# Last stage of a five-part transformer kernel: scores in 64x32 tiles, values in 64x64 tiles, one sine operation, value transfers two at a time, new orders of the work

## The chip, the cores and the metric

The kernel runs on one core of a Trainium2 chip. The metric is the time of one execution on the device in microseconds. Three runs of the kernel before gave a median of 4817.93 us (4815.92 to 4821.29).

## The reference

The input `x` is 16 sequences of 256 tokens with 128 features, in f32. Four blocks follow each other, each `x + attention(norm(x)) + ffn(norm(x))`. The change touches the second half of the last one alone (stage `L3f`), which has six layers:

```python
def attn_layer(x, Wqkv, qs, ksc, Wo):          # 16 heads of 64, INNER = 1024
    q, k, v = split(x @ Wqkv)
    q = l2norm(q) * qs;  k = l2norm(k) * ksc
    q = q * cos * scale + rotate_half(q) * sin * scale
    k = k * cos / scale + rotate_half(k) * sin / scale
    # windows of 32 tokens; each looks at its own 32 keys and the 32 before them
    sim = einsum('bhwie,bhwje->bhwij', bq, bk2) * 8.0      # 32 x 64 per head and window
    attn = softmax(where(mask, -max, sim))
    out = einsum('bhwij,bhwje->bhwie', attn, bv2)
    return out @ Wo
for i in range(6):
    x = attn_layer(shift_tokens(x), ...) + x
    x = ffn_layer(shift_tokens(x), ...) + x     # layer norm, 128 -> 2 x 341, gelu gate, -> 128
```

## The kernel before

Stages `L0`, `L1`, `L2`, `L3a` and `L3f` run one after the other on the one core. In `L3f` a unit `u` is one sequence in one layer, 6 x 16 = 96 units. A unit has two tiles `t` of 128 tokens. All matmuls are in f32; the profile has two records of a weight load and two of a matmul for each of them, one for each pass.

Each engine has an order of its work written out by hand in `pe(i)`, `act(i)`, `dve(i)` and `pool(i)`, for two units at a time: `i` counts pairs, and one call of each function issues what belongs to units from `2i - 1` to `2i + 4`. The engines meet in semaphores alone (`wait_ge`, `then_inc`). So the work runs as a software pipeline whose period is one value of `i`. SyncE's queue (`sp(k)`) moves the values and loads weights.

What a unit does, with the functions that the change and the prediction name:

- TensorE `project` makes q, k and v in twelve pieces of 128 x 512 (`"q0a"` is q, tile 0, first half) into three PSUM banks in turn.
- ScalarE `squared`, VectorE `sums` and `bounded`, ScalarE `length` and VectorE `norm` make the l2 norm and write q and k to `raw`.
- GpSimd `sine`, `cosine` and `add` rotate them in place. `sine` multiplies the two halves of each head crosswise, in two operations of 512 elements; `cosine` and `add` are one operation of 1024 each.
- TensorE `turn_qk` transposes four 128 x 128 pieces, ScalarE `turned` copies them out: k to `kT`, q to `qz`. `qz` holds each pair of heads twice as wide as needed: one head's 64 rows have values in 32 columns, the other's in the next 32, and the rest is zero from the start (a memset). So one matmul of 128 rows and 64 columns of weights gives both heads of a pair for one window of 32 queries.
- TensorE `scores` makes eight pairs times four windows of these, on two column tiles of 64.
- VectorE `hidden` (mask), `top` (maximum), `below` (difference), ScalarE `exponent`, VectorE `total`, `share` and `scale` are the softmax, on 1024 elements a partition.
- TensorE `turn_p` transposes, ScalarE `spread` copies in four pieces to `pT`, again with zeros between the heads.
- SyncE moves the values from `v2` to `vw` by windows, 16 transfers a unit (`sp`); TensorE `values` multiplies them with `pT`, 32 matmuls a tile, each with 128 rows, 64 columns of weights and 64 moving columns.
- ScalarE `output`, TensorE `project_out`, VectorE `residual`, then the feed-forward part: `centre`, `variance`, `centred`, `root`, `normal`, `affine`, `ffn_gate`, `gelu`, `ffn_up`, `gated`, `ffn_out`, `ffn_done`.

Two functions of stage L1 serve as comparison further on. Its `values` (lines 896 and 899) puts out to four column tiles of 32 in turn, its `scores` (line 857) takes from four row tiles of 32 in turn:

```python
for i in range(RG):   # RG = 4, rows(i) is the i-th group of 32 partitions
    p.matmul(PS[rows(i), 4, t * P:(t + 1) * P], vz[:, b, t, i, u * RW:(u + 1) * RW], sT[:, i, ...], ...)
    mm = p.matmul(PS[:, i, ...], km[rows(i), b, u, ...], qT[rows(i), b, ...], start=True, stop=True)
```

## Time and profile before

| | |
|---|---|
| median of three runs | 4817.93 us (4815.92 to 4821.29) |
| span of the profiled execution, first to last instruction | 4799.2 us |
| TensorE busy, of the span | 4554.0 us (95%) |
| VectorE | 3761.7 us (78%) |
| GpSimd | 3692.6 us (77%) |
| ScalarE | 3501.1 us (73%) |

The profile is of one execution. Its own time outside the span is not recorded; the median of the runs lies 18.7 us above the span. PE is TensorE's matmuls, PEld its weight loads, DVE is VectorE, ACT ScalarE, POOL GpSimd, SP SyncE. Each matmul's duration contains the way through the array, so a duration is longer than the time from one matmul to the next. The chain of waits is the chain of work that ended last, followed back from the end. `qz` stands as L3f_qz, and so on; PSUM is `ps`.

### The profile page before, as it was taken

What the parts mean: (1) busy time and instruction counts of PE and PEld (TensorE: products, weight loads), DVE (VectorE), ACT (ScalarE), POOL (GpSimd) and SP (SyncE); (2) the same over time, 40 slices, a digit from 0 to 9 for tenths busy, and PEclk for the clock granted to TensorE, in tenths of its full rate; (3) what the DMA queues carried; (4) which work ended last, traced back from release to release, by engine and by line L of the source; (5) the groups of instructions that cost most, each with busy time, mean ns of one, the idle gap of its engine ahead of it and who ended that gap; (6) DMA issues with size and microseconds to landing.
All of it is one profiled execution on the core that took longest, in us unless ns stands there. A gap on an engine that the chain in (4) does not pass through costs nothing.

```text
span 4799.2 us, 114895 instructions
## 1 busy us (share of the span) xinstructions
PE 4554.0 (95%) x44512; PEld 3128.6 (65%) x44512; DVE 3761.7 (78%) x5226; ACT 3501.1 (73%) x6738; POOL 3692.6 (77%) x2336
## 2 busy tenths in 40 slices
PE   7998999987887799999999999999999999999997
PEld 5666768874443466666666666666666666666665
DVE  6776556658999688888888888888888888888885
ACT  3454756557775688888888888888888888888885
POOL 2222334438998999999999999999999999999993
PEclk9898999998999999999999999999999999999998
DMA  2000000004332222232222322232322322322222
GB/s 79 1 2 1 2 1 1 1 1 168 150 142 106 55 63 63 56 85 70 54 67 65 75 68 55 68 75 61 68 64 67 76 53 66 80 64 63 62 56 52
DMA packets 164292, 289.06 MB, mean 60 GB/s; under 512 B 44063, under 2 KB 61351, under 8 KB 159655
## 3 DMA queue, kind: packets, MB, share of 16 engines
q1 hardware_dynamic: 162310, 281.46, 22.3%
q8 instruction: 357, 5.85, 0.5%
q14 instruction: 185, 1.51, 0.1%
q10 hardware_dynamic: 1440, 0.24, 0.0%
HBM read 90.22 MB, written 2.62 MB: 19 GB/s over the span
## 4 chain that ended last, share of the span: by engine, by line
PE 59%; ACT 3%; issue 2%; DVE 1%; POOL 1%; ACTq 0%; DVEq 0%; POOLq 0%
PE ps L2559 18%; PE ps L2614 8%; PE ps L2588 8%; PE ps L2572 7%; PE ps L2627 7%; PE ps L2601 3%; PE ps L2669 3%; PE ps L2660 3%; PE ps L2653 3%; ACT L3f_pT L2820 2%; PE ps L2634 1%; PE ps L2640 1%; ACT L3f_kT L2803 1%; POOL L3f_t L3155 0%; POOL L3f_raw L3172 0%
## 5 line engine op out<-in xcount | busy, mean ns | idle before, releaser
L3155 POOL TENSOR_TENSOR L3f_t<-L3f_raw,L3f_rot 128x512 f32<-128x512 f32 x768 | 1007.7, 1334 | 268.3 <-DVE L3f_raw L2971 268.3
L2559 PE MATMUL ps<-L3f_wqkv,all_z 128*128 128x512 f32 x2304 | 1133.7, 601 | 12.8 <-DVE L3f_raw L2971 11.7
L3172 POOL TENSOR_TENSOR L3f_raw<-L3f_raw,L3f_t 128x1024 f32<-128x1024 f32 x384 | 961.4, 2504 | 3.8
L3164 POOL TENSOR_TENSOR L3f_raw<-L3f_raw,L3f_rot 128x1024 f32<-128x1024 f32 x384 | 953.8, 2484 | 3.8
L2971 DVE TENSOR_TENSOR L3f_raw<-ps,L3f_ri 128x512 f32<-128x512 f32 x768 | 495.6, 682 | 231.9 <-ACT L3f_ri L2778 230.2
L2954 DVE TENSOR_REDUCE L3f_ss<-L3f_sqr 128x8 f32<-128x512 f32 x768 | 507.8, 681 | 163.2 <-ACT L3f_sqr L2768 160.8
L2572 PEld LDWEIGHTS ps<-all_ident,L3f_raw 128*128 128x128 f32 x3072 | 358.7, 141 | 320.7 <-issue 282.8
L2559 PEld LDWEIGHTS ps<-L3f_wqkv,all_z 128*128 128x128 f32 x2304 | 385.2, 191 | 221.0 <-issue 151.5
L2572 PE MATMUL ps<-all_ident,L3f_raw 128*128 128x128 f32 x3072 | 472.3, 276 | 49.1 <-ACT L3f_kT L2803 27.1
L2820 ACT ACTIVATE L3f_pT<-ps 64x512 f32<-64x512 f32 x768 | 453.2, 590 | 83.9 <-PE ps L2601 75.9
L2768 ACT ACTIVATE L3f_sqr<-ps 128x512 f32<-128x512 f32 x768 | 449.9, 599 | 76.5 <-PE ps L2559 71.7
L2799 ACT ACTIVATE L3f_qz<-ps 64x512 f32<-64x512 f32 x768 | 451.5, 588 | 59.7 <-PE ps L2572 55.2
L2614 PEld LDWEIGHTS ps<-L3f_pT,L3f_vw 128*64 128x64 f32 x12288 | 377.4, 139 | 95.4 <-issue 50.9
L2614 PE MATMUL ps<-L3f_pT,L3f_vw 128*64 128x64 f32 x12288 | 404.0, 225 | 7.5 <-ACT L3f_pT L2820 7.5
L2588 PEld LDWEIGHTS ps<-L3f_kT,L3f_qz 128*64 128x64 f32 x12288 | 375.2, 138 | 52.5 <-issue 52.5
L2588 PE MATMUL ps<-L3f_kT,L3f_qz 128*64 128x64 f32 x12288 | 399.1, 223 | 0.0
L2803 ACT ACTIVATE L3f_kT<-ps 128x512 f32<-128x512 f32 x384 | 231.9, 604 | 164.7 <-PE ps L2572 163.5
L2627 PE MATMUL ps<-L3f_oT,L3f_wo 128*128 128x256 f32 x1536 | 349.3, 381 | 2.6 <-ACT L3f_oT L2830 2.6
L2627 PEld LDWEIGHTS ps<-L3f_oT,L3f_wo 128*128 128x128 f32 x1536 | 292.9, 191 | 84.5 <-issue 46.2
L3014 DVE TENSOR_TENSOR L3f_sm<-L3f_sm,L3f_sl 128x1024 f32<-128x1024 f32 x192 | 339.3, 1767 | 0.0
L2281 POOL TENSOR_TENSOR L3a_db_x<-L3a_dx,L3a_Bs 128x1024 f32<-128x1024 f32 x128 | 299.4, 2358 | 1.3 <-DMA L3a_Bs<-L3a_rows 1.1
L1916 PE MATMUL ps<-L3a_hc,all_ident 128*128 128x512 f32 x512 | 248.7, 633 | 39.0 <-DVE L3a_hc L2189 22.5
(333 smaller groups left out, 8702.0 us busy)
## 6 DMA issues: line engine op xcount, KB each, us to landing
L3f_vw<-L3f_v SPq DMA_DIRECT2D x1344, 128.0 KB, 2.4
L3a_Bs<-L3a_rows SPq DMA_DIRECT2D x16, 2048.0 KB, 7.1
L3a_Cs<-L3a_rows SPq DMA_DIRECT2D x16, 2048.0 KB, 11.6
L3f_vw<-L3f_v SPq DMA_DIRECT2D x192, 64.0 KB, 2.1
L3f_wqkv<-in_L_ffn_Wqkv SPq DMA_DIRECT2D x24, 256.0 KB, 2.9
L3f_wqkv<-in_L_ffn_Wqkv SPq DMA_DIRECT2D x6, 512.0 KB, 3.6
L3f_wo<-in_L_ffn_Wo SPq DMA_DIRECT2D x48, 64.0 KB, 2.3
out<-all_x SPq DMA_DIRECT2D x8, 256.0 KB, 3.6
```

Source lines behind the costliest of these rows:

```text
L2559: p.matmul(PS[:, j % 3, :], Z[:, u % NSEQ, t * P:t * P + P], w, start=True, stop=True).then_inc(proj.sem)
L2572: mm = p.transpose(PS[:, 3, c * P:c * P + P], raw[:, t, (4 * g + c) * P:(4 * g + c + 1) * P], ident[:, :])
L2588: mm = p.matmul(PS[r, 6 + w // 2, a * KEYS:(a + 1) * KEYS], qz[:, t, a, w, :, :].rearrange("p h q -> p (h q)"), kT[:, a, t * P + w * WIN:t ...
L2614: mm = p.matmul(PS[r * HD:(r + 1) * HD, 4 + c // 2, (c % 2) * 256 + w * HD:(c % 2) * 256 + (w + 1) * HD], vw[:, u % 2, t * NW + w, a * HD: ...
L2627: mm = p.matmul(PS[:, 4, 0:SEQ], wo[:, c, h, :], oT[:, :, c, :, h, :], start=(c + h == 0), stop=(c + h == PAIRS // 2))
L2799: op = a.activation(qz[r, t, 4 * g:4 * g + 4, :, half, :], src[r, :, :].rearrange("p c (w q) -> p c w q", q=WIN), ACT.Copy)
L2820: op = a.activation(pT[half * HD:(half + 1) * HD, t, r:2 * PAIRS:2, :, half, :], PS[r * HD:(r + 1) * HD, 4:6, :].rearrange("p b (n w h q) ...
L2954: v.tensor_reduce(ss[:, 0, i * UH:(i + 1) * UH], heads(sqr[:, i % 2, :]), AX.X, ALU.add).then_inc(ss_in.sem)
L2971: v.tensor_tensor(heads(raw[:, t, g * UNIT:(g + 1) * UNIT]), heads(PS[:, RING.index(x) % 3, :]), ri[:, i * UH:(i + 1) * UH].unsqueeze(2).b ...
L3155: op = g.tensor_tensor(t[:, :, to], r[:, :, fr], w[:, 1, to].unsqueeze(1).broadcast_to((P, H, WIN)), ALU.mult)
L3164: g.tensor_tensor(r, r, w[:, 0, :].unsqueeze(1).broadcast_to((P, H, HD)), ALU.mult).then_inc(cosined.sem)
L3172: g.tensor_tensor(r, r, t, ALU.add).then_inc(rotated.sem)
```

## The change

- `qz` becomes `qT` without zeros: `turned` copies q in one operation. `scores` makes, for each pair, window and head, one matmul with 64 rows, 32 columns of weights and 64 moving columns: 64 a tile instead of 32. Window `w` puts out to column group `w`, head `h` takes row group `h` and writes to bank `6 + h`. The mask is laid out accordingly, and `below` writes `sm` in the order pair, head.
- `pT` has no zeros either: `spread` is one copy of 1024 elements. `values` makes, for each head, window and half, one matmul with 64 rows, 64 columns of weights and 32 moving columns: 64 a tile instead of 32, on two row and two column groups. `oT` and `project_out` follow its layout.
- The memsets of `qz` and `pT` go.
- `sine` is one operation of 1024 elements that reads the two halves of a head in reversed order.
- SyncE waits before each value transfer from the third on until the transfer two before it has landed, with two semaphores in turn.
- The orders of all four engines are written anew from the same functions, and `i` runs from -4 to N / 2 + 2 instead of -2 to N / 2.

```diff
-        qz = self.sb("qz", [P, TILES, PAIRS, NW, 2, WIN])
+        qT = self.sb("qT", [P, TILES, PAIRS, P])
-        pT = self.sb("pT", [P, TILES, 2 * PAIRS, 2, 2, WIN])
-        oT = self.sb("oT", [P, TILES, PAIRS // 2, NW, 2, WIN])
+        pT = self.sb("pT", [P, TILES, PAIRS, P])
+        oT = self.sb("oT", [P, TILES, 2, PAIRS // 2, P])
...
+                pieces = [(part, shift, half, w) for part, shift in ((WIN, 0), (0, 1)) for half in range(2) for w in range(NW)]
+                for n, (part, shift, half, w) in enumerate(pieces):
+                    landed = v_put[k % 2][n % 2]
+                    if n >= 2:
+                        s.wait_ge(*landed.at(k // 2, 16 * (n // 2) - 1))
...
                 for a in range(PAIRS):
                     for w in range(NW):
-                        r = slice(w % 2 * HD, w % 2 * HD + HD)
-                        mm = p.matmul(PS[r, 6 + w // 2, a * KEYS:(a + 1) * KEYS], qz[:, t, a, w, :, :].rearrange("p h q -> p (h q)"),
-                                      kT[:, a, t * P + w * WIN:t * P + w * WIN + KEYS], start=True, stop=True)
+                        for h, (r, _) in enumerate(halves):
+                            mm = p.matmul(PS[w * WIN:(w + 1) * WIN, 6 + h, a * KEYS:(a + 1) * KEYS], qT[r, t, a, w * WIN:(w + 1) * WIN],
+                                          kT[r, a, t * P + w * WIN:t * P + w * WIN + KEYS], start=True, stop=True)
...
                 for c in range(PAIRS // 2):
                     for w in range(NW):
-                        for r in range(2):
-                            a = 2 * c + r
-                            mm = p.matmul(PS[r * HD:(r + 1) * HD, 4 + c // 2, (c % 2) * 256 + w * HD:(c % 2) * 256 + (w + 1) * HD],
-                                          vw[:, u % 2, t * NW + w, a * HD:(a + 1) * HD],
-                                          pT[:, t, w // 2 * PAIRS + a, w % 2, :, :].rearrange("p h q -> p (h q)"), start=True, stop=True)
+                        for to, n in halves:
+                            a = 2 * c + n
+                            for h, (r, _) in enumerate(halves):
+                                mm = p.matmul(PS[to, 4 + h, c * P + w * WIN:c * P + (w + 1) * WIN], vw[r, u % 2, t * NW + w, a * HD:(a + 1) * HD],
+                                              pT[r, t, a, w * WIN:(w + 1) * WIN], start=True, stop=True)
...
-                    for half in range(2):
-                        r = slice(half * HD, half * HD + HD)
-                        op = a.activation(qz[r, t, 4 * g:4 * g + 4, :, half, :], src[r, :, :].rearrange("p c (w q) -> p c w q", q=WIN), ACT.Copy)
+                    op = a.activation(qT[:, t, 4 * g:4 * g + 4, :], src, ACT.Copy)
...
-                for r in range(2):
-                    for half in range(2):
-                        op = a.activation(pT[half * HD:(half + 1) * HD, t, r:2 * PAIRS:2, :, half, :],
-                                          PS[r * HD:(r + 1) * HD, 4:6, :].rearrange("p b (n w h q) -> p (b n) w h q", w=2, h=2, q=WIN)[:, :, :, half, :], ACT.Copy)
-                op.then_inc(pT_in.sem)
+                a.activation(pT[:, t, :, :].rearrange("p a q -> p (a q)"), PS[:, 4:6, :].rearrange("p b n -> p (b n)"), ACT.Copy).then_inc(pT_in.sem)
...
-                for half in range(2):
-                    to, fr = slice(half * WIN, (half + 1) * WIN), slice((1 - half) * WIN, (2 - half) * WIN)
-                    op = g.tensor_tensor(t[:, :, to], r[:, :, fr], w[:, 1, to].unsqueeze(1).broadcast_to((P, H, WIN)), ALU.mult)
-                op.then_inc(sined.sem)
+                g.tensor_tensor(t.rearrange("p h (b e) -> p h b e", b=2), r.rearrange("p h (b e) -> p h b e", b=2)[:, :, ::-1, :],
+                                w[:, 1, :].rearrange("p (b e) -> p b e", b=2).unsqueeze(1).broadcast_to((P, H, 2, HD // 2)), ALU.mult).then_inc(sined.sem)
...
-        for i in range(-2, N // 2 + 1):
+        for i in range(-4, N // 2 + 3):
```

## Rows read from the trace of the kernel before

**Rows 1.** The page: busy time of each engine.
```profile
PE 4554.0 (95%) x44512; PEld 3128.6 (65%) x44512; DVE 3761.7 (78%) x5226; ACT 3501.1 (73%) x6738; POOL 3692.6 (77%) x2336
```
**Rows 2.** Chain of waits, L3f: start us, us, what; period marks and bursts.
```profile
1677.77 3.45 PE ps L2627 x16
...
3064.14 3.45 PE ps L2627 x16
3067.59 0.44 PE ps L2572 x4
...
3071.49 2.02 PE ps L2588 x64
...
3079.15 2.02 PE ps L2614 x64
3081.16 1.87 PE ps L2588 x64
...
3130.08 3.45 PE ps L2627 x16
...
4712.15 3.73 PE ps L2627 x16
```
**Rows 3.** Busy time by stretch, one period: length, PE, PEld, DVE, ACT, POOL, clock, DMA.
```profile
3064.14:3130.08 65.94, 65.28 (x715) 44.84 (x715) 54.30 (x78) 53.85 (x102) 60.00 (x33) 1.00 0.34 85
```
**Rows 4.** Waits of POOL from 1700 to 4600 us: us in total, times, longest.
```profile
POOL L3f_t L3155 <- DVE L3f_raw L2971: 251.9, 171, 2.9
```
**Rows 5.** Timeline of TensorE's matmuls in stage L1: start us, us.
```profile
541.67 0.40 PE L899 MATMUL ps<-L_sT,L_onz 128*32 128x128 f32 x8
541.89 0.40 PE L896 MATMUL ps<-L_sT,L_vz 128*32 128x128 f32 x8
...
545.04 1.17 PE L857 MATMUL ps<-L_qT,L_km 32*128 32x128 f32 x32
```
**Rows 6.** Line 896 in 30 ns: records under way, PE (x), PEld (x).
```profile
541.42:541.46 0.03, 0.02 (x4) 0.03 (x4) 1.00 0.00 0
```
**Rows 7.** Weight loads by line, ns min/median/max: 32, 64 and 128 columns.
```profile
L896 PEld LDWEIGHTS ps<-L_sT,L_vz x512: 106/110/110, 480.3 to 634.4; 128*32 128x32 f32 x171
L2614 PEld LDWEIGHTS ps<-L3f_pT,L3f_vw x12288: 132/138/227, 1627.7 to 4766.1; 128*64 128x64 f32 x199
L857 PEld LDWEIGHTS ps<-L_qT,L_km x512: 181/187/333, 472.9 to 627.5; 32*128 32x128 f32 x171
```
**Rows 8.** Groups by line, ACT, the period of rows 3: busy us, mean ns.
```profile
L2820 ACT ACTIVATE L3f_pT<-ps 64x512 f32<-64x512 f32 x16 | 9.4, 590 | 1.7 <-PE ps L2601 1.5
L2799 ACT ACTIVATE L3f_qz<-ps 64x512 f32<-64x512 f32 x16 | 9.4, 588 | 1.2 <-PE ps L2572 1.1
...
L2830 ACT ACTIVATE L3f_oT<-ps 128x1024 f32<-128x1024 f32 x4 | 4.1, 1026 | 0.8 <-PE ps L2614 0.7
```
**Rows 9.** Timeline of POOL, the period before: start us, us; undisturbed operations.
```profile
3019.55 2.51 POOL L3155 TENSOR_TENSOR L3f_t<-L3f_raw,L3f_rot 128x512 f32<-128x512 f32 x2
...
3024.34 2.36 POOL L3164 TENSOR_TENSOR L3f_raw<-L3f_raw,L3f_rot 128x1024 f32<-128x1024 f32 x1
```
**Rows 10.** Groups by line, VectorE, the period of rows 3.
```profile
L3014 DVE TENSOR_TENSOR L3f_sm<-L3f_sm,L3f_sl 128x1024 f32<-128x1024 f32 x4 | 7.1, 1782 | 0.0
```
**Rows 11.** SP: one unit's issues, landing time, and its queue's waits.
```profile
3033.73 10.24 SPq L2510 DMA_DIRECT2D L3f_vw<-L3f_v  x16
...
L3f_vw<-L3f_v SPq DMA_DIRECT2D x1344, 128.0 KB, 2.4
...
SPq L2504 <- PE ps L2614: 1317.8, 88, 18.0
SPq L2510 <- ACT L3f_v L2787: 484.4, 44, 11.5
```
**Rows 12.** Chain of waits at the stage's start, and ACT in the last 99 us.
```profile
1556.91 3.47 DVE L3f_pT L3203
...
L2820 ACT ACTIVATE L3f_pT<-ps 64x512 f32<-64x512 f32 x20 | 11.8, 591 | 5.4 <-PE ps L2601 5.2
```

More of the change, by code:

```diff
@@ L2785, in value @@
                 if u >= 2:
-                    a.wait_ge(*v_put[u % 2].all(u // 2 - 1))
+                    for e in range(2):
+                        a.wait_ge(*v_put[u % 2][e].all(u // 2 - 1))
                 a.activation(v2[:, u % 2, int(x[1]), "ab".index(x[2]), :], PS[:, j % 3, :], ACT.Copy).then_inc(v_out.sem)
@@ L2872, in gelu @@
                     a.preload_act_table_set(EXP_LN)
+            value(2 * i + 1, "v0b")
+            squared(2 * i + 1, "q1a")
+            turned(2 * i, 1, 2)
+            squared(2 * i + 1, "q1b")
+            squared(2 * i + 1, "k1a")
+            length(2 * i + 1, "q1")
+            output(2 * i - 1, 0)
+            turned(2 * i, 1, 3)
+            squared(2 * i + 1, "k1b")
+            spread(2 * i - 1, 1)
+            length(2 * i + 1, "k1")
+            turned(2 * i + 1, 0, 0)
+            value(2 * i + 1, "v1a")
@@ new lines, in act @@
+            exponent(2 * i, 0)
+            turned(2 * i + 1, 0, 1)
+            affine(2 * i - 2)
+            value(2 * i + 1, "v1b")
+            squared(2 * i + 2, "q0a")
+            squared(2 * i + 2, "q0b")
+            output(2 * i - 1, 1)
+            squared(2 * i + 2, "k0a")
+            exponent(2 * i, 1)
+            length(2 * i + 2, "q0")
+            turned(2 * i + 1, 0, 2)
+            squared(2 * i + 2, "k0b")
+            turned(2 * i + 1, 0, 3)
+            centred(2 * i - 1)
@@ new lines, in act @@
+            length(2 * i + 2, "k0")
+            turned(2 * i + 1, 1, 0)
+            root(2 * i - 1)
+            value(2 * i + 2, "v0a")
+            turned(2 * i + 1, 1, 1)
+            squared(2 * i + 2, "q1a")
+            spread(2 * i, 0)
+            squared(2 * i + 2, "q1b")
+            value(2 * i + 2, "v0b")
+            turned(2 * i + 1, 1, 2)
+            output(2 * i, 0)
+            turned(2 * i + 1, 1, 3)
+            length(2 * i + 2, "q1")
+            exponent(2 * i + 1, 0)
+            spread(2 * i, 1)
@@ L3071, in dve @@
             bounded(2 * i + 3, "q0")
-            scale(2 * i + 1, 1)
+            sums(2 * i + 3, "k0a")
+            normal(2 * i)
             norm(2 * i + 3, "q0a")
+            share(2 * i + 1, 1)
             norm(2 * i + 3, "q0b")
-            normal(2 * i)
             land(2 * i - 1, range(FINAL - 1))
```

319 lines of the change are left out of this document (136 added, 183 removed).

## The prediction

> **What bounds the kernel now.** I read the page first: its busy shares [rows 1] show a kernel in which TensorE is busy 95% of the span and three other engines over 70%, so no share alone names the bound. The changed stage L3f runs from about 1.56 ms to the end, and there the chain of waits repeats itself: the same 16-record piece of `project_out` stands at 3064.14 and 3130.08 us [rows 2], so one pass of the written-out orders (two sequences, a "period" below) takes 65.94 us. From 1677.77 to 4712.15 us that is 3034.38 / 65.94 = 46.0 periods. The busy time by stretch [rows 3] says what fills one: TensorE 65.28 us at a granted clock of 1.00, GpSimd 60.0, VectorE 54.3, ScalarE 53.85. TensorE idles 0.66 us; GpSimd idles 5.9, and the waits [rows 4] show it waiting for VectorE's `norm` and for nothing else. So TensorE's work sets the period, and GpSimd stands 9% behind it.
>
> **Scores.** A record is one of the two passes that an f32 matmul takes. Now `scores` makes 32 matmuls, 64 records, with 64 weight columns and 64 moving columns, on two column tiles in turn. Four such bursts stand in a period: three of 2.02 us and one of 1.87 [rows 2], 7.93 us in all. The short one follows `values`, which has the same tile shape, so entering a shape costs 0.15 us, and in the steady burst a record takes 1.87 / 64 = 29.2 ns; the two tiles together take 58.4 ns for a round of two. After the change there are 64 matmuls, 128 records, of 32 weight and 64 moving columns, and eight tiles (two row groups, four column groups) come in turn. Do eight work at once? The L1 stage is the nearest row [rows 5]. `L896` and `L899` use four column tiles with 128 moving columns: 8 records from 541.67 to 541.89 us, 27 ns a record, 110 ns a round of four. A pass of 128 columns by itself takes the same 110 ns (`L2572`, four in 0.44 us [rows 2]): four column tiles cost no more than one. `L857` uses four row tiles: 32 records of 128 columns in 1.17 us, 37 ns each with entry and exit instead of 110, so row tiles overlap as well. And tiles can start close together: four matmul records and four weight loads begin inside one stretch of 30 ns [rows 6], about 7 ns from tile to tile, which puts eight of them into some 56 to 60 ns. A round of eight should then take what a round of two takes now, 58.4 ns. 128 / 8 = 16 rounds make 0.93 us, with the entry 1.09. Four bursts: 7.93 to 4.36, **-3.6 us a period**. Bounds: the best is this very value, since a tile's own 64 columns can't go faster; the worst is that no average below the 27.3 ns of [rows 5] can be had, 128 x 27.3 = 3.5 us a burst.
>
> **Values.** The same doubling: 64 records become 128, the moving side shrinks from 64 to 32 columns, but each load still brings 64 weight columns, now to four tiles. What a load costs is in the durations [rows 7]: 110 ns for 32 columns, 138 for 64, 187 for 128, so 0.8 ns a column on top of a fixed part, and 64 columns are some 52 ns. A tile that needs new weights for each record thus can't have a record more often than every 52 ns, whatever its moving side is. I take the round at today's 58.4 ns: 128 / 4 = 32 rounds make 1.87 us, with the entry 2.02. Four bursts: 8.08 to 8.08, **0**. Bounds: 32 rounds at half, 29 ns, are 0.93 + 0.15 = 1.09 us (-3.7 a period), if the load hides; 3.5 us a burst (+5.9 a period) if 27.3 ns is the least.
>
> The skill has a rule that promises more here than the rows do: the Trainium skill, "TensorEngine Tiling (Array Packing)", section "Theoretical Speedup", gives up to twofold for each dimension of 64 or less, by which `values`, going from column tiles to row and column tiles with the same total work, would halve. By it the sum below would be about 4.53 ms, by the load durations it is 4.65 ms. Its warning beside this, not to take a tiling factor from a dimension that is small already (section "Instruction Overhead"), is on the side of the durations.
>
> **ScalarE.** In a period sixteen half-height copies of `qz` (9.4 us) become eight of full height, at today's 0.59 4.7 us, and sixteen of `pT` (9.4 us) become four of 1024 elements at 1.03, 4.1 us [rows 8]: 53.85 to 44 us, -9.9. ScalarE isn't the bound, so I count nothing, but latencies on TensorE's side shrink: `spread` from 2.4 us to 1.03. At most TensorE's 0.66 us of idle time can be won by it.
>
> **VectorE.** `hidden`, `below`, `total`, `scale` keep their 1024 elements; `below` now writes in another order, which no row prices. It costs from 0 to, if it took the price of the dearest of them twice (`L3014`, 1.78 [rows 10]), some +1.8 x 4 = 7 us: 54.3 would be 61.5, still behind TensorE's 61.7. I take 0, since its element count stays.
>
> **GpSimd.** The two 512-element products of `sine` take 2.51 us together when undisturbed, a 1024-element one 2.36 [rows 9]. One operation saves 0.15, eight times a period: -1.2, GpSimd 60.0 to 58.8. The reversed order of halves is in no row; at worst it gives that back, for more than 2.51 nothing in the rows speaks. It is hidden now, and it matters as the next bound.
>
> **Value transfers.** Sixteen transfers are issued in 10.24 us, one each 0.64, and one takes 2.4 us to land [rows 11]. With two in flight a pair costs 2.4 to 2.5: 8 x 2.45 = 19.6 us a sequence, +9.4. Behind the waiting SP instruction stand the next sequence's transfers and the layer's weight loads. SP waits 1318 + 484 = 1802 us in 88 sequences now, 20.5 each, so it has room for 9.4. The burst issued at 3033.73 serves `values` at 3079.15, 45 us later [rows 2, 11]; 19.6 is in time. It would decide only from 31 us a sequence, 3.9 us a pair. The weights of the next layer, issued behind them, could come up to 4 us later, five times in all: I take 0, at most 20 us in the whole run.
>
> **Orders.** The new orders hold the same operations. TensorE at 65.28 - 3.57 = 61.7 us needs GpSimd to be busy 58.8 of 62.4, and VectorE to feed it: GpSimd's idle share shrinks from 5.9 to 3.6 us a period. The price of an order is in no row of before. It lies between -0.66 us (no idle time left) and +3.6 us (the whole gain given back); I keep today's 0.66 us idle, the nearest row.
>
> **Head and tail.** The `pT` memset of 3.47 us is on the chain at 1556.91 [rows 12] and goes: -3.5. In the last 99 us the twenty `pT` copies take 11.8 us and there is little else to cover them; five full ones take 5.2. I take some 60% of them for being on the chain, -4, and three score bursts -3. Together -10.
>
> **Sum.** Period 61.7 + 0.66 = 62.4, 3.54 less; x 46.0 = -163; head and tail -10: -173. The profiled execution has a span of 4799.2; the median of the runs is 4817.93, so 18.7 us lie around the span. 4799.2 - 173 + 18.7 = **4645 us**.
>
> **Rivals.**
> - *A: as summed*, 4645, own range 4600 (0.5 us less idle and a cheaper entry) to 4700 (1.2 us a period more waiting). Chance 0.56.
> - *B: `values` gains too.* The load hides behind the other tiles' work. Then TensorE needs 61.7 - 3.7 = 58.0, GpSimd's 58.8 takes over as bound, and with 1.2 us of its waiting left the period is 60.0: 5.9 x 46 + 10 = 283 less, 4534. For it: a round of four column tiles already covers four loads. Against: the durations of [rows 7]. 0.12.
> - *C: a least time for each record; slower.* Twice as many records of half the work cost twice as much if TensorE can't average below some 27 ns. Place: both bursts. 3.5 + 3.5 us instead of 2.02 + 2.02, less the 0.15 of the short one: (28.0 - 16.0) = +12 a period, x 46 = +550, so 5360 us with the 10 of head and tail. It decides from a mean of 16.0 / 1024 = 15.6 ns a record (the sum above has 12.44 / 1024 = 12.1). For it: no stretch of the trace is denser than 27.3 ns. Against: that stretch is explained by its 128 columns over four tiles, and starts 7 ns apart show [rows 6]. 0.15. The Trainium skill, "TensorE: Matmul & The Clock Gate", section "Wait — 56ns, not 53.3ns?", speaks for this rival: matmuls never start less than about 25 ns apart, however small; by its figure the sum would be some 5.25 ms. Its own section "The mechanism" has tiles start about 4 ns apart, and the 30 ns stretch of this trace agrees with that one.
> - *D: no more than four tiles at once*, the most that a row shows. Scores then take 32 rounds, 1.87 + 0.15, and TensorE's work stays: the change does nothing to the bound; head and tail remain, 4810. 0.09.
> - *E: the new orders bring waits* between VectorE, GpSimd and TensorE that take back 2.5 to 4.5 us a period: 4760 to 4850. For it: GpSimd at 94% of the period instead of 91%. 0.08.
>
> **Numbers.** The likeliest gives 4645. From 4530 (B) to 4815 (D, half of E) lie 0.56 + 0.12 + 0.09 + 0.04 = 0.81; C is left out above. A difference of 0.2%, 10 us, is about what this measurement can tell. Faster: A, B, a third of D and E, 0.74. Same: 0.07. Slower: C and the rest, 0.19.
>
> **What would show it.** The period between two 16-record `project_out` pieces: 62.4. `scores` in the chain: 128 records in about 1.1 us (3.5 under C, 2.0 under D). `values`: 2.0 (1.1 under B). ScalarE 44 us a period, GpSimd 58.8. TensorE's waits still small; under B and E, waits for GpSimd's or VectorE's tiles at `L2572` and `L2559`. No wait for `v_put`. I am wrong above all if eight small tiles don't overlap, since nothing in this trace has run eight.

## The result and the profile after

The change made the kernel slower: 5036.25 us (median of 4, 5035.66 to 5068.0) against 4816.93, ratio 1.0481, 95% interval 1.0453 to 1.0508. The forecast was 4645, in a range of 4530 to 4815: the time went the other way, to a place outside that range. One run of e11 below (5209 us) and one of e13 (8369 us) took far longer than the rest at a lower granted clock; the ratios leave them out, and the medians hardly move by them. The profiled execution has a span of 5034.3 us; at the same marks as in [rows 2] its period is (4955.75 - 1670.23) / 46 = 71.4 us, 5.5 more than before and 9.0 more than forecast.

The page of the changed kernel, busy time of each engine and the queue that brings instructions (packets, MB, share of 16 engines' span); it answers to [rows 1]:

```profile
PE 4554.6 (90%) x69088; PEld 3037.0 (60%) x69088; DVE 3839.6 (76%) x5225; ACT 3259.4 (65%) x5964; POOL 3674.7 (73%) x1951
...
q8 instruction: 549, 8.99, 0.7%
```

TensorE executes half as many records again and is idle 10% of the span, 5% before. Before, the same queue moved 357 packets and 5.85 MB. A packet is 8.99 MB / 549 = 16 KB. TensorE's compiled program has 8995584 bytes, 549.05 times 16 KB, in instructions of 64 bytes each: the queue brings TensorE's instructions, 256 in a packet. A packet's time is 0.7% x 5034.3 x 16 / 549 = 1.0 us.

Busy time by stretch of the changed kernel, one of the better periods (columns as in [rows 3]):

```profile
3027.79:3097.19 69.40, 63.71 (x1228) 42.46 (x1227) 56.74 (x78) 48.98 (x86) 60.57 (x26) 1.00 0.26 59
```

Even here TensorE idles 5.7 us, for 0.66 before, at a granted clock of 1.00. The chain of waits of the changed kernel shows two places. First the bursts of small tiles (start us, us, what):

```profile
3083.46 2.00 PE ps L2619 x128
...
3089.07 1.41 PE ps L2591 x91
...
3114.51 1.39 PE ps L2591 x84
3115.89 1.23 issue
3117.12 0.34 PE ps L2591 x12
3117.46 1.91 PE ps L2562 x4
3119.38 2.00 PE ps L2619 x128
```

`values` (L2619) takes 2.00 us for 128 records, as forecast for it (2.02). `scores` (L2591) takes 1.41 where nothing is wrong, and at 3115.89 it has a hole of 1.23 us *inside one burst*, released by nothing that the profile shows. The chain lists only some of a burst's records (the trace has all 128), so a burst is to be read by its times here, not its counts. A "hole" is a step of over 0.6 us from the start of one record of a burst to the start of the next. Measured in the trace from a burst's first record to the next operation, over the 192 bursts, in us:

```
          scores: shortest   mean   holes over 0.6 us   values: median   mean   holes
before               1.97    2.01                   0             2.02   2.03       0
after                1.40    1.89                  47             2.00   2.09       3
```

Second, right behind it, the gelu and its table loads. The chain of waits of the changed kernel, and ScalarE's timeline over the same time:

```profile
3121.44 1.11 PE ps L2657 x2
...
3123.16 1.01 ACT L3f_oT L2830
...
3124.20 1.28 ACT L2814
3125.49 1.06 ACT L3f_sm L2814
3126.55 0.48 ACT L3f_v L2792
...
3127.05 1.28 ACT L2780
...
3131.40 0.70 ACT L3f_gg L2870
...
3132.14 1.57 PE ps L2664 x2
```

```profile
3119.17 1.28 ACT L2866 ACT_TABLE_LOAD   x1
3122.58 0.69 ACT L2870 ACTIVATE L3f_gg<-ps,L3f_b 128x512 f32<-128x512 f32 x1 [2.12 <-PE ps L2657]
...
3124.20 1.28 ACT L2814 ACT_TABLE_LOAD   x1
...
3127.05 1.28 ACT L2780 ACT_TABLE_LOAD   x1
...
3128.58 1.28 ACT L2782 ACT_TABLE_LOAD   x1
...
3130.11 1.28 ACT L2870 ACT_TABLE_LOAD   x1
3131.40 1.26 ACT L2870 ACTIVATE L3f_gg<-ps,L3f_b 128x512 f32<-128x512 f32 x2
3132.68 1.28 ACT L2872 ACT_TABLE_LOAD   x1
```

The new ScalarE order puts `exponent` and `length` between the first gelu and the other two. These functions live in different activation tables, so ScalarE loads six tables a period in place of two; two of the six stand inside `length`, whose two functions (L2780, L2782) now get a load each. TensorE fills the time behind the first gelu with `project_out` and then stands still at `ffn_up`'s second part (L2664) until the second gelu comes. Its timeline, with the idle time before the operation in brackets:

```profile
3124.95 3.62 PE L2631 MATMUL ps<-L3f_oT,L3f_wo 128*128 128x256 f32 x16
3132.14 1.57 PE L2664 MATMUL ps<-L3f_fn,L3f_w 128*128 128x512 f32 x2 [3.57 <-ACT L3f_gg L2870]
```

The waits of the changed kernel from 1700 to 4850 us (total, times, longest) show it in sum, 3.5 us in each of 44 periods; before TensorE never waited for a gelu:

```profile
PEld ps L2664 <- ACT L3f_gg L2870: 171.3, 44, 4.0
PE ps L2664 <- ACT L3f_gg L2870: 153.7, 44, 3.6
```

A third loss stands in no chain: what such a wait leaves behind. The trace has two levels of TensorE's granted clock, 1.2 and 2.4 GHz (0.50 and 1.00). The busy time by stretch, of the kernel before and of the changed one:

```profile
1700.00:4700.00 3000.00, 2968.86 (x32403) 2036.23 (x32404) 2480.44 (x3512) 2447.92 (x4590) 2731.29 (x1455) 1.00 0.28 66
```

```profile
1700.00:4850.00 3150.00, 2884.12 (x53945) 1894.15 (x53944) 2481.57 (x3400) 2158.57 (x3744) 2631.75 (x1056) 0.97 0.27 62
```

From 1600 us on, the clock rows of the trace have 209 us at the lower level in the changed kernel and 33 in the one before. 36 of the 45 stretches behind 1700 us begin within 2 us of the end of a wait for the second gelu. At half the clock up to half of the time is lost, so this part can be worth up to (209 - 33) / 2 = 88 us of the 219 that the change cost (an estimate: it takes TensorE to be busy all the while). The experiment e3 below shows it most clearly.

### The profile page after: what moved, and what is told of

Read it like the earlier page. It is cut to its first block, busy times and chain, and to the rows that moved or that the text cites. A ratio compares the mean times of both kernels' runs of the same rounds, so it can differ in the third digit from the quotient of the medians.

```text
span 5034.3 us, 162887 instructions
## 1 busy us (share of the span) xinstructions
PE 4554.6 (90%) x69088; PEld 3037.0 (60%) x69088; DVE 3839.6 (76%) x5225; ACT 3259.4 (65%) x5964; POOL 3674.7 (73%) x1951
## 3 DMA queue, kind: packets, MB, share of 16 engines
q8 instruction: 549, 8.99, 0.7%
## 4 chain that ended last, share of the span: by engine, by line
PE 50%; ACT 8%; issue 6%; DVE 4%; POOL 1%; ACTq 0%; DVEq 0%; POOLq 0%
PE ps L2562 19%; PE ps L2619 7%; PE ps L2575 6%; PE ps L2591 5%; PE ps L2631 3%; PE ps L2664 3%; PE ps L2604 3%; PE ps L2673 2%; DVE L3f_sm L3015 1%; PE ps L2657 1%; ACT L2870 1%; ACT L2780 1%; ACT L2814 1%; ACT L3f_oT L2830 1%; ACT L3f_sm L2814 1%
## 5 line engine op out<-in xcount | busy, mean ns | idle before, releaser
L3154 POOL TENSOR_TENSOR L3f_t<-L3f_raw,L3f_rot 128x1024 f32<-128x1024 f32 x384 | 941.2, 2451 | 510.7 <-DVE L3f_raw L2971 510.7
L2619 PEld LDWEIGHTS ps<-L3f_pT,L3f_vw 64*64 64x64 f32 x24576 | 380.5, 135 | 126.2 <-issue 114.5
L3015 DVE TENSOR_TENSOR L3f_sm<-L3f_sm,L3f_sl 128x1024 f32<-128x1024 f32 x192 | 451.0, 2349 | 0.1
L2619 PE MATMUL ps<-L3f_pT,L3f_vw 64*64 64x32 f32 x24576 | 404.2, 220 | 7.8 <-issue 4.9
L2591 PE MATMUL ps<-L3f_kT,L3f_qT 64*32 64x64 f32 x24576 | 302.0, 225 | 71.2 <-issue 69.5
L2591 PEld LDWEIGHTS ps<-L3f_kT,L3f_qT 64*32 64x32 f32 x24576 | 262.6, 105 | 148.6 <-issue 147.8
L2664 PE MATMUL ps<-L3f_fn,L3f_w 128*128 128x512 f32 (+1 forms) x288 | 196.0, 771 | 160.8 <-ACT L3f_gg L2870 160.8
L2802 ACT ACTIVATE L3f_qT<-ps 128x512 f32<-128x512 f32 x384 | 227.9, 593 | 166.9 <-PE ps L2575 161.2
L2981 DVE TENSOR_TENSOR ps<-ps,L3f_lmaskb 128x1024 f32<-128x1024 f32 x192 | 235.8, 1228 | 85.5 <-PE ps L2591 85.1
L3037 DVE SCALAR_TENSOR_TENSOR L3f_gg<-ps,L3f_b,L3f_gg 128x512 f32<-128x512 f32 x144 | 107.8, 749 | 248.7 <-PE ps L2664 248.4
```

The costliest lines, as they stand in the source:

```text
L2591: mm = p.matmul(PS[w * WIN:(w + 1) * WIN, 6 + h, a * KEYS:(a + 1) * KEYS], qT[r, t, a, w * WIN:(w + 1) * WIN], kT[r, a, t * P + w * WIN:t ...
L2619: mm = p.matmul(PS[to, 4 + h, c * P + w * WIN:c * P + (w + 1) * WIN], vw[r, u % 2, t * NW + w, a * HD:(a + 1) * HD], pT[r, t, a, w * WIN:( ...
L3015: v.tensor_tensor(x, x, sl[:, t, :].unsqueeze(2).broadcast_to((P, H, KEYS)), ALU.mult).then_inc(s_mul.sem)
L3154: g.tensor_tensor(t.rearrange("p h (b e) -> p h b e", b=2), r.rearrange("p h (b e) -> p h b e", b=2)[:, :, ::-1, :], w[:, 1, :].rearrange( ...
```

## The experiments

All times are medians; the kernel before, run beside them, had 4805 to 4817 us. The column "L3f" has the time from the first record of `project` in the changed stage to the end, in the one profiled execution of each kernel; before has 3243. It is a check on small differences: the stages ahead are the same in all kernels, yet the first `project` of L3f stands anywhere from 1547 to 1588 us.

| kernel | us | ratio to before (95%) | L3f | mean scores burst, holes |
|---|---|---|---|---|
| after | 5036 | 1.048 (1.045 to 1.051) | 3479 | 1.89, 47 |
| e1 after, gelus together | 4937 | 1.026 (1.022 to 1.030) | 3363 | 1.88, 42 |
| e2 after, orders of before | 4911 | 1.022 (1.019 to 1.026) | 3338 | 2.32, 86 |
| e3 before, orders of after | 5224 | 1.087 (1.084 to 1.090) | 3663 | |
| e15 e3, gelus together | 5065 | 1.054 (1.051 to 1.057) | 3509 | |
| e4 e2, transfers of before | 4886 | 1.017 (1.014 to 1.020) | 3326 | 2.32, 83 |
| e12 before, transfers of after | 4817 | 1.000 (0.998 to 1.002) | 3250 | |
| e11 before, one sine operation | 4808 | 0.998 (0.996 to 1.000) | 3240 | 2.00, 0 |
| e5 small scores alone | 4768 | 0.990 (0.987 to 0.993) | 3207 | 1.93, 52 |
| e6 small values alone | 4858 | 1.009 (1.006 to 1.012) | 3291 | 2.12, 12 |
| e7 e4, scores in late quarters | 5346 | 1.110 (1.106 to 1.113) | 3779 | 16 |
| e8 e5, scores in late quarters | 5306 | 1.101 (1.097 to 1.105) | 3756 | 0 |
| e9 e5, scores in early halves | 4850 | 1.008 (1.005 to 1.010) | 3294 | 38 |
| e10 e5, scores in early quarters | 5051 | 1.050 (1.046 to 1.053) | 3486 | 5 |
| e13 e5, bursts at good places | 4763 | 0.991 (0.988 to 0.993) | 3200 | 1.57, 7 |
| e14 e5, bursts at bad places | 4901 | 1.019 (1.017 to 1.022) | 3341 | 2.03, 58 |
| e16 e13, cheaper padding | 4733 | 0.984 (0.982 to 0.986) | 3173 | 1.63, 12 |

**The orders: e1, e2, e3, e15.** e1 changes two lines of ScalarE's order:

```diff
             gelu(2 * i - 1, 0)
+            gelu(2 * i - 1, 1)
+            gelu(2 * i - 1, 2)
             output(2 * i, 1)
             exponent(2 * i + 1, 1)
             value(2 * i + 2, "v1a")
             length(2 * i + 2, "k1")
-            gelu(2 * i - 1, 1)
-            gelu(2 * i - 1, 2)
```

> The changed kernel with the three gelu calls of a period next to each other again on ScalarE (the changed order has an exponent, a value copy and a length between the first and the second). Theory O (the new ScalarE order is the main loss): six table loads a period become two, 5.1 us of ScalarE, and TensorE's wait of some 9 us at ffn_up falls to under 4; the period of 71.5 us falls to 65 to 67, the time to 4770 to 4860 us. Theory T (the small tiles are the main loss, through more instructions): the wait moves but the time stays over 4980 us.

e2 has the functions of after and the four orders of before, e3 the reverse; both take the loop's range along. e15 is e3 with the edit of e1.

> The changed kernel (small tiles, one sine operation, transfers two at a time) with all four orders of before. Theory O: the loss is in the orders, so this lands at 4780 to 4830 us, near before, since the score bursts of the changed kernel take 1.89 us on average and so win next to nothing over the 2.01 of before. Theory T: over 4980 us. My prediction's mechanism, had the orders been harmless, would give 4645.

> The kernel before with the four new orders alone (large tiles, two sine operations, free transfers). Theory O: 4990 to 5080 us, as slow as the changed kernel or slower, with six table loads a period. Theory T: 4800 to 4850 us.

> The functions of before with the four new orders, but the three gelu operations side by side (as in the run of that name): the new orders on the large tiles without the added table loads. They cost 100 us in the changed kernel (5036 to 4937) and the rest of the new orders nothing there (4937 against 4911 with the old ones). Theory: most of the 409 us that the new orders cost on the large tiles is the table loads and what waits behind them: 4830 to 4950. Rival O (the new orders fit only the shorter ScalarE operations of the new tiles, since ScalarE has 54 us of work in 66 here): above 5000 even without the table loads.

Splitting the gelus costs 99 us in the changed kernel (5036 to 4937) and 159 on the large tiles (5224 to 5065). Not all of this is waiting. TensorE's timeline of e3, the same line ahead of the wait and behind it:

```profile
1781.04 1.02 PE L2660 MATMUL ps<-L3f_fn,L3f_w 128*128 128x512 f32 x2
...
1789.09 2.08 PE L2660 MATMUL ps<-L3f_fn,L3f_w 128*128 128x512 f32 x2 [3.57 <-ACT L3f_gg L2870]
```

The same two records take twice as long: from 1788.00 to 1794.80 us the granted clock is 0.50, and such a stretch stands in every period. From 1600 us on e3 has 346 us at the lower level and e15 104, the changed kernel 209 and e1 128. By the estimate used above the clock is up to 121 of the 159 us and up to 40 of the 99.

The rest of the new orders costs 26 us in the changed kernel (4937 against 4911) and 254 on the large tiles (5065 against 4811): rival O of the last text holds there. TensorE's waits from 1700 to 4600 us, first in e15, then in e1:

```profile
PE ps L2627 <- ACT L3f_oT L2830: 92.3, 41, 2.3
PE ps L2614 <- ACT L3f_pT L2820: 49.0, 41, 1.2
PE ps L2572 <- ACT L3f_qz L2799: 37.3, 40, 1.2
```

```profile
PE ps L2631 <- ACT L3f_oT L2830: 94.5, 42, 2.3
```

The waits for the copies of p and q are there with the large tiles alone, whose copies take longer. e1's wait for `output` costs less than it says, for e1 has 42 holes where e2, without that wait, has 86: while TensorE waits for an engine, its next instructions can arrive. All four times missed what was set: e1 came 77 us above its range, e3 144 above, e15 above theory's 4950 and in its rival's place, and e2 81 above. In e2 a hole can now be in `values` too (20 of 192, 3 in the changed kernel). The chain of waits of e2:

```profile
2030.08 1.99 PE ps L2619 x126
2032.07 0.46 issue
2032.53 0.24 PE ps L2619 x2
...
2051.03 0.67 PE ps L2591 x46
2051.70 1.99 issue
2053.69 1.38 PE ps L2591 x74
```

**Transfers and sine: e4, e12, e11.** e4 takes the wait for the transfer before last out of e2; e12 and e11 put the new transfers, and the new sine, into the kernel before and nothing else.

```diff
-                    if n >= 2:
-                        s.wait_ge(*landed.at(k // 2, 16 * (n // 2) - 1))
```

> As e2_old_orders, but the value transfers are issued without waiting for each other. If bursts of transfers hold up the fetch of TensorE's instructions, the gaps inside the score bursts grow and the time is 10 to 50 us above e2_old_orders. If waiting two by two has no effect on the rest, the two agree within 5 us.

> The kernel before with the one edit of the value transfers (two at a time on two semaphores each, in place of sixteen issued at once). By the difference of the two versions with old orders (4911 with the wait, 4886 without) it costs 0 to 30 us here; a rival in which fewer transfers at once leave the instruction packets more room gives 10 to 20 us less than before, but before has no idle stretch at such packets to win back.

> The kernel before with the one edit of the sine (one GpSimd operation for two halves). GpSimd is busy 60 of 66 us a period and behind TensorE. Theory: within 0.3% of before, 4795 to 4820; a rival in which GpSimd's rotation decides when the turns of q and k start gives 4750 to 4790, about 1 us a period.

e4 is 26 us faster than e2, and neither of the two outcomes that I had set (10 to 50 us slower, or within 5) came. In the kernel before the paced transfers cost 1 us. But of the 27 us between the two profiled executions of e2 and e4 15 lie ahead of L3f; inside the stage the transfers cost 12 us there (3338 against 3326) and 7 in the kernel before (3250 against 3243). So a small cost is likely, and that it arises with small tiles alone isn't shown. The sine is worth 7 us at most, 3 inside the stage, at the edge of what the measurement can tell.

**Which tile: e5, e6.** Both stand on e4. e5 puts the large value tiles back, with the small tiles' `scores`:

```diff
-                        for to, n in halves:
-                            a = 2 * c + n
-                            for h, (r, _) in enumerate(halves):
-                                mm = p.matmul(PS[to, 4 + h, c * P + w * WIN:c * P + (w + 1) * WIN], vw[r, u % 2, t * NW + w, a * HD:(a + 1) * HD],
-                                              pT[r, t, a, w * WIN:(w + 1) * WIN], start=True, stop=True)
+                        for r in range(2):
+                            a = 2 * c + r
+                            mm = p.matmul(PS[r * HD:(r + 1) * HD, 4 + c // 2, (c % 2) * 256 + w * HD:(c % 2) * 256 + (w + 1) * HD],
+                                          vw[:, u % 2, t * NW + w, a * HD:(a + 1) * HD],
+                                          pT[:, t, w // 2 * PAIRS + a, w % 2, :, :].rearrange("p h q -> p (h q)"), start=True, stop=True)
...
+                for r, half in halves:
+                    for b in range(2):
+                        op = a.activation(pT[r, t, b * PAIRS:(b + 1) * PAIRS, :, half, :],
+                                          PS[r, 4:6, :].rearrange("p c (n b w q) -> p (c n) b w q", b=2, w=2, q=WIN)[:, :, b, :, :], ACT.Copy)
```

e6 puts the large score tiles, `qz` and the old mask back and keeps the small values, with eight copies of a quarter each for the turned p.

> The orders and transfers of before, the one sine operation, scores in 64x32 tiles, but values again in 128x64 tiles with zero halves (64 large ones a burst, four copies out of the PSUM for the turned p). Theory F (TensorE runs dry of instructions: a scores burst is 128 weight loads and 128 matmuls, run off in a little over 1 us, and the next 16 KB of instructions land later than that): the scores burst keeps gaps of 1 to 2.5 us in a third or more of the bursts, and the time is that of the version with both kinds of small tiles and the old orders (4886) within 30 us: 4850 to 4915. Rival V (it is the small value tiles that lose the time, their doubled records make the instructions scarce for what follows): the gaps in scores all but vanish, the mean burst is near 1.4 us, and with 4 x 0.5 us a period won the time is 4690 to 4760.

> The orders and transfers of before, the one sine operation, values in 64x64 tiles without zero halves, but scores again in 128x64 tiles (64 a burst). Theory F: a values burst is now 256 instructions in 2.0 us, a little faster than the instructions come, so some bursts get a gap of up to 1 us but far fewer than the scores had; TensorE's work is that of before: 4815 to 4870. Rival V: the loss of the small tiles sits here, 4870 to 4920. A third view, that less ScalarE work alone helps, would give 4780 to 4810.

For e5 rival V is nearly right in the time, 4768 for its 4690 to 4760 and 118 us less than e4, and wrong in what the bursts do: it has them at 1.4 us, and 52 holes stay, more than a quarter of the bursts, as under F. The small value tiles bring nothing by themselves (2.00 us for 2.02) and double their share of the instructions. From e4 to e5 the scores bursts in sum fall from 444.6 to 370.4 us and the values bursts from 420.6 to 396.3, 98 of the 118. e6 is slower than before and inside F's range; 12 of its bursts of large scores have a hole, which none has in the kernel before, and 7 of its `values`; its eight small ScalarE copies are part of that, so its 49 us aren't the price of the tiles alone. e5 beats the kernel before by 1.0%.

**Are the holes a lack of instructions? e7 to e10.** The burst is issued in parts; only the placing differs. Late: the first part where the burst was, the others each behind a later operation. Early: the last part where the burst was.

```diff
-            scores(2 * i + 2, 0)
+            scores(2 * i + 2, 0, 0)
             project(2 * i + 3, "v0b")
+            scores(2 * i + 2, 0, 1)
             project(2 * i + 3, "q1a")
+            scores(2 * i + 2, 0, 2)
             project(2 * i + 3, "q1b")
+            scores(2 * i + 2, 0, 3)
```

> The version with the old orders and free transfers (4886), where each burst of 128 small scores is issued in four parts of 32 with another operation of TensorE between each two. The same instructions, only spread over more time. Theory F: no stretch of 256 instructions is run off in much under 2.5 us any more, so idle stretches of over 0.6 us inside scores fall from some 80 to under 20 and their total from some 170 us to under 60; what the later last part costs in waits for the masks is smaller: 4760 to 4840. Rival D (the records themselves are slow, by bank or by tile conflicts, wherever they stand): the parts add up to as much as the whole burst did, and the later scores come on top: 4886 to 4960.

> Small scores in four parts as in the run before it, and large values with zero halves as in the first of these runs: the lowest number of TensorE instructions with small scores. Theory F: as few gaps as with quarters and both small tiles or fewer, since values issue half as many instructions: 4720 to 4810, the fastest of these four. Rival D: 4880 to 4960.

> The version with small scores alone (4768), with each burst in two halves of 64. The second half stays where the burst was; the first (pairs 0 to 3, which need one copy fewer of the turned q and k) stands one or two operations of TensorE earlier, before a turn, a projection or the values. So the last score is no later than before, and a stretch of 256 instructions takes some 1.6 us in place of 1.1. Theory F: idle stretches of over 0.6 us inside scores fall from 52 to 15 to 35, and nothing else is late: 4700 to 4760. Rival L (what the run in late quarters lost was the price of any split, not of the later last part): above 4790.

> Small scores alone, in four parts of 32, the last of them where the burst was and the first three one operation each earlier (before the values of the other tile two and two). Theory F: under 15 idle stretches of over 0.6 us are left inside scores; the parts start up to 1.5 us earlier and may wait for the bank that the masks and maxima of the tile before still hold, up to 0.5 us a burst: 4680 to 4760. Rival L: above 4790, as in the late quarters (5306).

In the scores the holes went down, 83 to 16 in e7 and from 52 to 0, 38 and 5 in e8, e9 and e10, as F says but for e9, which it had at 15 to 35. Some only moved: `values` has 31 in e7 for 18 in e4, and 14 in e9 for none in e5, so e9 has 52 in all, as many as e5. The times went the other way. It isn't rival D: a part of 32 records takes 0.39 us in the median of e7, the four 1.56. Two more ends of the scores show. What the scores of e7 waited for and who waited for them (us, times):

```profile
  ACT L3f_qT L2814: 36.4, 48
who waited for it (us, times):
  DVE ps L2993: 729.5, 192
```

VectorE's mask waits 3.8 us for each late burst (729.5 / 192; in e4 it is 55.8 / 192 = 0.3). And what the scores of e10 waited for, besides issue:

```profile
  DVE L3f_sm L3013: 143.3, 47
  ACT L3f_kT L2820: 55.5, 41
  DVE all_z L3064: 47.8, 46
```

An early part waits for the bank that `below` of the tile before still reads (L3013), for the other one that the FFN's residual still reads (L3064), and for k. I had priced this at 0.5 us a burst at most; it is (143.3 + 55.5 + 47.8) / 192 = 1.3. My forecast for all four was wrong by 90 us and more. Rival L's number was met too. Its price of any split wasn't told apart from these waits; what the rows show is that a burst has a window, between the bank's release before it and the mask behind it, and that the spread parts reach beyond it on either side.

**The same instructions at other places: e13, e14.** A sharper test had to leave the order alone. In e5's compiled program I counted at which place each burst starts, in blocks of 256 TensorE instructions from the program's start:

```
start within the block     bursts   holes   mean burst, us
0 to 63                        49       8     1.76
64 to 127                      43       5     1.68
128 to 191                     49       3     1.56
192 to 255                     51      36     2.66
```

The same count gives the place at which each hole ends, and that is sharper still: all 52 holes of e5 end at place 195 or 196, and so do all 47 of the changed kernel, the 7 of e13, the 58 of e14 and the 12 of e16, wherever their bursts start. There TensorE goes over from one packet's instructions to the next's.

e13 pads a period with some 20 tiny matmuls to a multiple of 256 instructions, so that each burst keeps its place, and e14 is e13 but for one number, 47 where e13 has 30.

```diff
+                first = 30 if (u, x) == (0, "q0a") else 0
+                for n in range(first + (u >= 2) * {"q1b": (1 - u % 2) * 7, "k1b": (1 - u % 2) * (13 - u // 2 % 2)}.get(x, 0)):
+                    p.matmul(PS[0:WIN, j % 3, 0:2], ident[0:HD, 0:WIN], ident[0:HD, 0:2], start=True, stop=True)
                 p.matmul(PS[:, j % 3, :], Z[:, u % NSEQ, t * P:t * P + P], w, start=True, stop=True).then_inc(proj.sem)
```

> Small scores alone (4768) with some 20 tiny matmuls of 2 columns more a period (78 instructions), put ahead of projections whose bank they write first. They make a period of TensorE's program 8 times 256 instructions long, so that each of the four scores bursts of a period always starts at the same place within a 16 KB block of 256 instructions; 30 more of them at the very start choose the places: about 183, 134, 108 and 66. In the kernel without them 36 of the 52 bursts with an idle stretch over 0.6 us were among the 50 that start at 192 to 255, and few among those at 64 to 191. Theory F (a block that is asked for when the block before it is entered comes in 2 to 3 us after, and what is ahead runs out before only if the burst starts just behind that point): fewer than 15 such stretches in 192 bursts, the mean burst falls from 1.93 to 1.5 to 1.65 us, the tiny matmuls cost 10 to 25 us, the time is 4705 to 4760. Rival R (the stretches come from something else that only happens in bursts, such as the clock or tile changes): as many as before, 4775 to 4800.

> The same kernel as the run before it but for one number: 47 in place of 30 tiny matmuls at the very start, so that the bursts start at about 251, 202, 176 and 134 within a block. Theory F: the first two bursts of nearly every period have an idle stretch over 0.6 us, 65 to 95 in 192, the mean burst is 2.1 to 2.5 us and the time is 60 to 130 us above that of the run before. Rival R: the same time as the run before within 0.3%.

What the scores waited for, first in e13, then in e14:

```profile
  ACT L3f_qT L2803: 36.4, 48
  issue: 34.1, 134
```

```profile
  issue: 206.9, 227
  ACT L3f_qT L2803: 36.4, 48
```

17 tiny matmuls at the start of a stage, some 1 us of work, make 138 us of difference at the end, 140 inside L3f. 88 of them are the longer scores bursts (389.7 us in sum for 301.6); another 28 are 36 idle stretches in `turn_p`, of which e13 has none. In e14, 46 of the 49 bursts that start at 192 to 223 have a hole, and none of the 95 that start at 64 to 191. The order and the work are the same, so rival R is out: it had the two within 0.3%.

The packets say how a hole comes about. In e14, 371 of the stage's 374 packets start only after TensorE has gone over place 195 into the block ahead of theirs, 1.2 us after that in the median. Where a hole follows, TensorE goes on 2.2 to 2.9 us after the packet's start in eight of ten cases. A burst that starts at 196 to 223 runs nearly the whole block in 1.4 us, and is at its end before the next block has come. A burst that starts at 64 to 191 goes over place 195 early, into a block whose packet started while slower work was still running (argued, but for the counts above).

e13's bursts and holes are as forecast (1.57 us, 7), its time 3 us above the range. e14's mean burst (2.03 us) and holes (58 for 65 to 95) are a little below theirs, since of the bursts at about 251, which should have had holes too, only 11 have one; the difference is a little above the 60 to 130.

**The padding's price: e16.** e13 had 45 holes fewer than e5 and 69 us less in its bursts, yet only 4 us less time. Busy time by stretch from 1700 to 4500 us, of e5 and of e13:

```profile
1700.00:4500.00 2800.00, 2729.36 (x41703) 1841.03 (x41704) 2335.06 (x3319) 2068.96 (x3996) 2531.76 (x1032) 1.00 0.29 68
```

```profile
1700.00:4500.00 2800.00, 2788.21 (x43384) 1895.95 (x43383) 2332.28 (x3322) 2076.05 (x3997) 2534.88 (x1033) 1.00 0.29 68
```

TensorE is busy 97.5% in e5 and 99.6% in e13: the holes were filled with padding. One after the other on one tile, the tiny records mostly started 32 ns apart, which for 1892 is 60 us. e16 spreads them over four tiles:

```diff
-                    p.matmul(PS[0:WIN, j % 3, 0:2], ident[0:HD, 0:WIN], ident[0:HD, 0:2], start=True, stop=True)
+                    r, c = halves[n % 2][0], (2 * (n % 2) + n // 2 % 2) * WIN
+                    p.matmul(PS[c:c + WIN, j % 3, 0:2], ident[r, 0:WIN], ident[r, 0:2], start=True, stop=True)
```

> The version with the bursts at the good places (4763), but with the tiny matmuls spread over four 64x32 tiles of the array in place of one. On one tile their records followed each other every 31.7 ns, 1892 of them or some 57 us of a TensorE that is busy 99.6% of the last stage, which is why the shorter bursts (1.57 us in place of 1.93, 69 us) gave nothing on the whole. Spread, they should follow every 8 to 16 ns as the scores do: 30 to 43 us less, 4720 to 4735. If their price was not what hid the gain, the time stays within 0.3% of 4763.

4733 us, as forecast and 1.6% under the kernel before: the best version of this study, small scores, large values, old orders, one sine, and bursts that don't start just behind place 195. The tiny records now start 9.4 ns apart in the mean (32.9 in e13).

## Why the prediction was wrong, step by step

The forecast of 4645 missed by 391 us. e4 tells how it divides: with the small tiles and the sine, but the old orders and transfers, the prediction's own mechanism should have given some 4645, and e4 has 4886. So 241 us are the tiles' side, 26 the transfers and 125 the orders. Measured against the kernel before, the orders are the larger loss (125 of 219), since the tiles, which were to win most of the forecast's 173 us, cost only 75.

- **Scores** is the step that failed by most: 1.09 us a burst in the sum, measured 1.89 in the changed kernel and 2.32 in e4. 4 x (2.32 - 1.09) is 4.9 us a period, 226 in 46 periods. Two things are in it. First, eight tiles do overlap, but a round of eight takes 80 ns and not 58.4. In a burst without a hole the first 32 records come 8.3 ns apart in the mean, with the 7 ns of [rows 6] from tile to tile inside a round, and the other 96 10.5 ns apart; with the way to the next operation that is 1.41 us. Second, and larger in e4, the holes. No term stood for the supply of instructions: the sum counted what the array does, not what has to be brought to it.
- **Orders** were bounded by -0.66 and +3.6 us a period and taken at nothing. Measured are 125 us, 2.7 a period, inside the bounds; on the large tiles 419 / 46 = 9.1 (5224 against 4805) is far outside. 99 of the 125 are the split gelus. The step said "the same operations"; it should have counted the table loads that the compiler adds wherever functions of different tables meet, six for two, 1.28 us each, and asked which one stands before an operation that TensorE waits for.
- **The clock** had no term either: the sum took every period at the 1.00 of [rows 3]. The waits that the orders brought, and the holes, lowered it (209 us at the lower level for 33), for which up to 88 us are an estimate.
- **Values** was right, 2.00 for 2.02 (2.09 in the mean), and with it the refusal of rival B and of the twofold gain. That the weight loads set this pace is the prediction's argument; no run here tells it apart from another cause. What it left out is the side effect: its doubled instructions cost the rest 118 us (e4 against e5, spread copies included).
- **Rival C** named the wrong price: 27 ns a record as a floor, where 1.41 us / 128 = 11 ns are seen. Its decision point was a mean of 15.6 ns over both kinds of bursts; measured are 4 x (1.89 + 2.09) / 1024 = 15.5, so by another road it came true as far as "no gain". The figure in the Trainium skill, "TensorE: Matmul & The Clock Gate", section "Wait — 56ns, not 53.3ns?", of about 25 ns between the starts of two matmuls, doesn't hold for small tiles side by side: the measurement is 11.
- **Rival D**, no more than four tiles at once, is out: by it a round of eight would take 117 ns, and it takes 80.
- **Rival E** had the right place for part of the loss (waits brought by the orders) but the wrong engine: it looked at GpSimd's share, while ScalarE, which the sum gave 44 us a period and thus no attention, made TensorE wait. The page can't warn of that; an engine at 65% can still stand last.
- **Value transfers** at nothing: 26 us by the medians of e2 and e4 and 12 inside their stage, 1 and 7 in the kernel before (e12), so wrong by little.
- **ScalarE** 44 us forecast; in the period shown 48.98, of which four table loads more than before are 4 x 1.28 = 5.1. **GpSimd**: one sine operation takes 2.45 us, forecast 2.36, and was worth 7 us at most (e11).
- **VectorE** was asked about the wrong operation. `below`, which now writes in another order, takes 1.20 us for 1.22, so nothing was right for it. `scale` (L3015) takes 2.35 us for [rows 10]'s 1.78 and stands on the chain at 3075.19, 4 x 0.58 = 2.3 us a period. The same function takes 1.75 in e2, with the orders of before, so the tiles alone don't lengthen it; with the new orders on the large tiles (e3) it is 1.96. Why isn't tested.

Accounted with the experiments: 4811 before; small tiles with the old orders +75 (e4, sine included), paced transfers +26 (e2), new orders without the split +26 (e1), the split +99: 5036 in sum, but for rounding. Inside L3f the same steps are 83, 12, 25 and 116. What stays open is why the records of a burst come 10.5 ns apart after the first 32, why e14's bursts at place 251 so rarely have a hole, and what lengthens `scale`.

## What to carry to other kernels

Before splitting TensorE's work into smaller tiles, count its instructions beside its cycles: a burst that executes a 16 KB block in less time than the next takes to come runs dry, and where it stands within the block then decides. Split only what gains by it (here scores, not values). Look at the granted clock behind each new wait: the wait's own length isn't all that it costs. When an order is laid out anew, read off which activation tables alternate, and never put another table's function between two that TensorE waits for; a reordering is tested alone, on the old functions too.

## What the runs showed of the hardware

- TensorE's instructions come in blocks of 256 (16 KB packets, 1.0 us each). A scores burst is 256 instructions in 1.4 us. A packet mostly starts after TensorE has entered the block before its own (e14: 371 of 374, 1.2 us after in the median), and TensorE goes on 2.2 to 2.9 us after the packet's start, so a hole can be 2 us and more.
- In these programs the blocks change at place 195 or 196, counted from the program's start: all 176 holes of the changed kernel, e5, e13, e14 and e16 end there. Bursts that start just behind it run dry (e14: 46 of 49 at 192 to 223).
- One constant in the program's head moved a 4.8 ms kernel by 138 us (4763 to 4901) with the same work.
- Records of eight 64x32 tiles in turn start 7 ns apart at best and 10 in the mean of a burst. Tiny matmuls of two columns start some 32 ns apart on one tile and 9.4 in the mean over four; the same 1892 records then cost 31 us less in the whole kernel (e13 to e16).
- In e3 TensorE's granted clock fell from 1.00 to 0.50 at 1788.00 us, within a wait of 3.57 us that ended at 1789.09, and stayed there to 1794.80; two records of the same line took 2.08 us in it for 1.02 before.
